# A recurrent block and an expert layer on one core: arithmetic moved off VectorE

## The reference, cut to what matters

```python
def wkv(k, v):                      # step over the 256 tokens of a sequence
    a = ew * a + exp(k_t) * v_t;  b = ew * b + exp(k_t)
    out_t = a / (b + 1e-8)
y  = layernorm(x);  xn = ln1(y)                        # two norms, one upon the other
k, v, r = mixes of (xn, shifted xn) @ Wk, Wv, Wr
x2 = y + (sigmoid(r) * wkv(k, v)) @ Wo
yn = ln2(x2);  kk = relu((yn + shifted yn) / 2 @ Wfk) ** 2
x3 = x + x2 + sigmoid(yn @ Wfr) * (kk @ Wfv)
m  = layernorm(x3);  scores = m @ gate                 # ln3
out = x3 + sum over the 2 best experts e of prob_e * w3_e(silu(h1) * h2),  h1, h2 = w12_e(m)
```

## Time and profile before

| | |
|---|---|
| median of three runs | 346.63 us (344.88 to 347.21) |
| the profiled execution | 347.12 us |
| its span, from the first to the last instruction | 345.2 us |
| busy of the span: TensorE, VectorE, GpSimd, ScalarE | 78%, 72%, 62%, 57% |
| first stage, until the last dispatch has landed | about 223 us |

### The profile page before, as it was taken

One profiled execution on the slowest core, in us unless ns is written; L12 is line 12 of the kernel. 1 busy time (PEld: TensorE's weight loads), 2 busy tenths in 40 slices (PEclk: granted clock), 3 DMA queues, 4 the chain that ended last, 5 costly groups with the idle time before them and its releaser, 6 DMA issues.

```text
span 345.2 us, 6699 instructions
## 1 busy us (share of the span) xinstructions
PE 269.8 (78%) x1697; PEld 209.4 (61%) x1698; DVE 249.8 (72%) x789; ACT 197.6 (57%) x413; POOL 215.4 (62%) x226
## 2 busy tenths in 40 slices
PE   0687599996967999695948734989999999999700
PEld 0233266673836757373745421689999999999700
DVE  3079998999889898997824648156666666666794
ACT  3546478786866588475535303366666666766200
POOL 5224356356767788588587677536666666666680
PEclk9999899999998799897896965899999999999965
DMA  8999900707162171301011211333333333333784
GB/s 273 434 316 381 353 0 2 277 4 292 41 223 92 32 293 48 93 31 61 26 39 54 70 41 47 85 90 90 94 90 88 91 90 85 84 99 92 256 313 173
DMA packets 30613, 46.11 MB, mean 134 GB/s; under 512 B 4333, under 2 KB 15599, under 8 KB 30336
## 3 DMA queue, kind: packets, MB, share of 16 engines
q1 hardware_dynamic: 23616, 30.76, 27.7%
q0 software_dynamic: 4352, 8.47, 7.4%
q10 hardware_dynamic: 2624, 6.64, 5.0%
HBM read 15.09 MB, written 29.18 MB: 128 GB/s over the span
## 4 chain that ended last, share of the span: by engine, by line
issue 30%; DVE 23%; POOL 22%; PE 5%; DMA 5%; SPq 1%; DVEq 1%; POOLq 1%; ACT 0%
POOL res_d L451 11%; POOL rows_d L426 7%; DVE st L832 4%; DVE den L883 2%; DVE rden L893 2%; DVE num L887 2%; DVE xm L937 2%; DMA o_all<-res_d 2%; DVE mv L839 2%; POOL rs L374 2%; POOL gated L389 1%; PE p_f L733 1%; DMA rows_d<-rows,pos 1%; DMA res_d<-yo,result_row 1%; DVE ekv L882 1%
## 5 line engine op out<-in xcount | busy, mean ns | idle before, releaser
L451 POOL DMA_INDIRECT res_d<-yo,result_row x72 | 71.5, 993 | 38.7 <-issue 29.6
L426 POOL DMA_INDIRECT rows_d<-rows,pos x64 | 67.3, 1052 | 22.8 <-issue 22.5
L806 PE MATMUL p_up<-xgT,w_up 128*128 128x128 f32 x576 | 70.2, 275 | 0.0
L806 PEld LDWEIGHTS p_up<-xgT,w_up 128*128 128x128 f32 x576 | 67.2, 192 | 0.0
L1062 DVE SCALAR_TENSOR_TENSOR gate_h<-th,p_up 128x512 f32<-128x512 f32 x36 | 24.8, 688 | 39.6 <-ACT th L610 39.6
L625 ACT ACTIVATE w_up<-w_exp 128x512 f32 x72 | 41.3, 622 | 10.1 <-DVE slot_w L1040 5.1
L721 PE MATMUL p_up<-ysum,w_sb 128*128 128x512 f32 x64 | 36.9, 687 | 5.3 <-POOL ysum L404 5.3
L610 ACT ACTIVATE th<-p_up 128x512 f32<-128x512 f32 x36 | 21.5, 597 | 28.1 <-PE p_up L806 28.1
L733 PEld LDWEIGHTS p_f<-wfv_half,kk 128*128 128x128 f32 x256 | 32.2, 198 | 5.3 <-issue 4.9
L733 PE MATMUL p_f<-wfv_half,kk 128*128 128x128 f32 x256 | 33.1, 283 | 0.0
L893 DVE RECIPROCAL rden<-den 128x512 f32<-128x512 f32 x8 | 26.7, 3343 | 0.0
(11 more groups left out here) (151 smaller groups left out, 550.8 us busy)
## 6 DMA issues: line engine op xcount, KB each, us to landing
rows_d<-pad SPq DMA_DIRECT2D x8, 2080.0 KB, 7.8
xg<-rows_d SPq DMA_DIRECT2D x72, 65.0 KB
o_all<-res_d SPq DMA_DIRECT2D x16, 256.0 KB, 5.2
w_exp<-experts ACTq DMA_DIRECT2D x1, 3072.0 KB, 16.9
x_all<-x SPq DMA_DIRECT2D x10, 256.0 KB, 2.4
out<-x_all ACTq DMA_DIRECT2D x8, 256.0 KB, 2.4
x_all<-x SPq DMA_DIRECT2D x1, 1536.0 KB, 15.8
res_d<-yo,result_row POOLq DMA_INDIRECT x72
```

The source lines that it names most:

```text
L426: pool.indirect_dma_start(out=rows_d[:, :], out_offset=bass.IndirectOffsetOnAxis(ap=row, axis=0), in_=rows_of[is_last(c)][:, t, k, :], in_ ...
L451: pool.indirect_dma_start(out=res_d[:, :], out_offset=bass.IndirectOffsetOnAxis(ap=row, axis=0), in_=yo[u][:, n, :], in_offset=None, bound ...
L806: mm = pe.matmul(p_up[u % 2][:, n, h * P:(h + 1) * P], w_up[u % 2][:, n, h * P:(h + 1) * P], xgT[u % 2][:, n, :], start=True, stop=True)
```

## The change

The moments' small arithmetic (neg1, var1, neg2, var2, var3) moves from VectorE to GpSimd, into the power steps. The copies in `moments` go: each `bn_aggr` now waits for its own `bn_stats`. The epsilon of den becomes a ScalarE step, `add_eps`, with a place of its own in ScalarE's order, ahead of `gate_y`. GpSimd's gated goes, and ScalarE's second instruction for tr: VectorE makes wkv = num * rden (`divided`, behind the reciprocal) and rw = (tr + 1) * wkv. `label` and `place` get by with fewer instructions; esum = 1 + egap moves to ScalarE. The loops of `pipeline` and of the first norms are written out, so that all chunk numbers are constants. Buffers that the moves need (two of each st, one mv1 for all chunks, a token_no for either place) are left out of this diff.

```diff
-            first, last = min(lags), CHUNKS - 1 + max(lags)
-            lo, hi = max(lags) + 1, CHUNKS - 1 + min(lags)
-
-            def turn(i):
+            for i in range(min(lags), CHUNKS + max(lags)):
                 for step, lag in steps:
-                    if not isinstance(i, int) or 0 <= i - lag < CHUNKS:
+                    if 0 <= i - lag < CHUNKS:
                         step(i - lag)
-
-            for i in range(first, lo):
-                turn(i)
-            with eng.Fori(lo, hi + 1) as i:
-                turn(i)
-            for i in range(hi + 1, last + 1):
-                turn(i)
...
-                pool.wait_ge(S["ln1_var"], last)
+                pool.wait_ge(S["ln1_moments"], last)
+                pool.tensor_scalar(neg1[:, part], mv1[:, part, 0], -1.0, None, ALU.mult)
+                pool.tensor_scalar(var1[:, 0, part], mv1[:, part, 1], LN_EPS, None, ALU.add)
+                pool.tensor_scalar(var1[:, 1, part], mv1[:, part, 1], 1.0 + LN_EPS, LN_EPS * LN_EPS, ALU.mult, ALU.add)\
+                    .then_inc(S["ln1_var"], 1)
+                pool.wait_ge(S["ln1_var"], n + 1)
...
+                after(pool, "ln2_moments", c + 1)
+                after(pool, "z2_ready", c)
+                pool.tensor_scalar(var2[:, :], mv2[:, :, 1], LN_EPS, None, ALU.add).then_inc(S["ln2_var"], 1)
+                pool.tensor_scalar(neg2[:, :], mv2[:, :, 0], -1.0, None, ALU.mult).then_inc(S["ln2_neg"], 1)
                 after(pool, "ln2_var", c + 1)
-                after(pool, "z2_ready", c)
                 pool.tensor_tensor(rs2[:, :], var2[:, :], neg_half[:, 0, 0:TPC], ALU.pow).then_inc(S["ln2_rstd"], 1)
+                after(pool, "ln2_neg", c + 1)
                 after(pool, "ln2_rstd", c + 1)
                 pool.tensor_tensor(nm2[:, :], rs2[:, :], neg2[:, :], ALU.mult).then_inc(S["nm2_ready"], 1)
...
-            def gate_sums(c):
-
-                after(pool, "gate_r1", c + 1)
-                after(pool, "num_ready", c + 1)
-                after(pool, "rw_ready", c)
-                pool.tensor_tensor(gated[:, :], tr[:, :], num[:, :], ALU.mult).then_inc(S["gated_ready"], 1)
...
+                after(pool, "ln3_moments", c + 1)
+                after(pool, "xm_ready", c)
+                pool.tensor_scalar(var3[:, :], mv3[:, :, 1], LN_EPS, None, ALU.add).then_inc(S["ln3_var"], 1)
                 after(pool, "ln3_var", c + 1)
-                after(pool, "xm_ready", c)
...
+            def add_eps(c):
+
+                after(act, "den_ready", c + 1)
+                act.activation(den[:, :], den[:, :], ACT.Identity, bias=wkv_eps[:, 0:1]).then_inc(S["den_eps"], 1)
+
             def tanh_r(c):
 
                 after(act, "r_done", c + 1)
-                after(act, "gated_ready", c)
+                after(act, "rw_ready", c)
                 act.activation(tr[:, :], p_r[:, :], ACT.Tanh, scale=0.5).then_inc(S["gate_r"], 1)
-                after(act, "gate_r", c + 1)
-                act.activation(tr[:, :], tr[:, :], ACT.Copy, bias=1.0).then_inc(S["gate_r1"], 1)
...
+                after(act, "egap_ready", c + 1)
+                act.activation(esum[:, :], egap[:, :], ACT.Copy, bias=1.0).then_inc(S["esum_ready"], 1)
...
-                           (first_apply, 0), (gate_y, 3), (first_norm, 2)])
+                           (first_apply, 0), (add_eps, 1), (gate_y, 3), (first_norm, 2)])
...
+                st = st[:, c % 2]
+                after(dve, which + "_moments", c - 1)
                 for t in range(TPC):
-                    last = dve.bn_stats(st[:, t, :], src(t))
-                last.then_inc(S[which + "_stats"], 1)
-                after(dve, which + "_stats", c + 1)
-
-                w = int(which[2]) - 1
-                dve.tensor_copy(moments_wait[:, w:w + 1], st[:, TPC - 1, 0:1])
+                    dve.bn_stats(st[:, t, :], src(t)).then_inc(S[which + "_stats"], 1)
                 for t in range(TPC):
-                    last = dve.bn_aggr(mv[:, t, :], st[:, t, :])
+                    after(dve, which + "_stats", c * TPC + t + 1)
+                    last = dve.bn_aggr(mv(t), st[:, t, :])
                 last.then_inc(S[which + "_moments"], 1)
-                after(dve, which + "_moments", c + 1)
...
-                moments(lambda t: x_all[:, bass.ds(c * TPC + t, 1), :].rearrange("p o d -> p (o d)"), st1, mv1, "ln1", c)
-                dve.tensor_scalar(neg1[:, tiles_of(c)], mv1[:, :, 0], -1.0, None, ALU.mult)
-
-
-                dve.tensor_scalar(var1[:, 0, tiles_of(c)], mv1[:, :, 1], LN_EPS, None, ALU.add)
-                dve.tensor_scalar(var1[:, 1, tiles_of(c)], mv1[:, :, 1], 1.0 + LN_EPS, LN_EPS * LN_EPS, ALU.mult, ALU.add)\
-                    .then_inc(S["ln1_var"], 1)
+                moments(lambda t: x_all[:, bass.ds(c * TPC + t, 1), :].rearrange("p o d -> p (o d)"), st1,
+                        lambda t: mv1[:, c * TPC + t, :], "ln1", c)
...
-                if last - first == 1:
-                    ln1(first)
-                else:
-                    with dve.Fori(first, last) as c:
-                        ln1(c)
+                for c in range(first, last):
+                    ln1(c)
...
+                after(dve, "rden_ready", c)
                 dve.tensor_tensor_scan(den[:, :], decay[:, :], ekf, 0.0, ALU.mult, ALU.add).then_inc(S["den_ready"], 1)
-                after(dve, "den_ready", c + 1)
-                dve.tensor_scalar(den[:, :], den[:, :], WKV_EPS, None, ALU.add).then_inc(S["den_eps"], 1)
                 after(dve, "ekv_ready", c + 1)
...
+            def divided(c):
+
+                after(dve, "rden_ready", c + 1)
+                after(dve, "num_ready", c + 1)
+                dve.tensor_tensor(wkv[:, :], num[:, :], rden[:, :], ALU.mult).then_inc(S["wkv_ready"], 1)
+
             def receptance(c):
 
-                after(dve, "gated_ready", c + 1)
-                after(dve, "rden_ready", c + 1)
+                after(dve, "wkv_ready", c + 1)
+                after(dve, "gate_r", c + 1)
                 after(dve, "wo_done", c)
-                dve.tensor_tensor(rw[:, :], gated[:, :], rden[:, :], ALU.mult).then_inc(S["rw_ready"], 1)
+                dve.scalar_tensor_tensor(out=rw[:, :], in0=tr[:, :], scalar=1.0, in1=wkv[:, :],
+                                         op0=ALU.add, op1=ALU.mult).then_inc(S["rw_ready"], 1)
...
-                moments(lambda t: x2[:, t, :], st2, mv2, "ln2", c)
                 after(dve, "nm2_ready", c)
-                dve.tensor_scalar(neg2[:, :], mv2[:, :, 0], -1.0, None, ALU.mult)
-                dve.tensor_scalar(var2[:, :], mv2[:, :, 1], LN_EPS, None, ALU.add).then_inc(S["ln2_var"], 1)
+                moments(lambda t: x2[:, t, :], st2, lambda t: mv2[:, t, :], "ln2", c)
...
-                moments(lambda t: x3[:, t, :], st3, mv3, "ln3", c)
                 after(dve, "ln3_rstd", c)
-                dve.tensor_scalar(var3[:, :], mv3[:, :, 1], LN_EPS, None, ALU.add).then_inc(S["ln3_var"], 1)
+                moments(lambda t: x3[:, t, :], st3, lambda t: mv3[:, t, :], "ln3", c)
...
-                for k in range(TOPK):
-                    last = dve.tensor_tensor(spots[:, k, :, :], hot[:, k, :, :], spot[:, :, :], ALU.mult)
-                last.then_inc(S["spots_ready"], 1)
+                dve.tensor_tensor(spots[:, :, :, :].rearrange("p k t e -> p k (t e)"),
+                                  hot[:, :, :, :].rearrange("p k t e -> p k (t e)"),
+                                  spot[:, :, :].rearrange("p t (o e) -> p o (t e)", o=1).to_broadcast([P, TOPK, TPC * E]),
+                                  ALU.mult).then_inc(S["spots_ready"], 1)
...
-                after(dve, "egap_ready", c + 1)
-                dve.tensor_scalar(esum[:, :], egap[:, :], 1.0, None, ALU.add).then_inc(S["esum_ready"], 1)
-
-                dve.tensor_tensor(higher[:, 0, :], low[:, 0, :], low[:, 1, :], ALU.is_lt)
-                dve.tensor_tensor(higher[:, 1, :], low[:, 1, :], low[:, 0, :], ALU.is_lt).then_inc(S["order_known"], 1)
-                after(dve, "order_known", c + 1)
-
+                dve.tensor_tensor(higher[:, :], low[:, 0, :], low[:, 1, :], ALU.is_lt).then_inc(S["order_known"], 1)
+                after(dve, "esum_ready", c + 1)
                 after_dispatched(dve, c)
                 rows = rows_of[is_last(c)]
+                dve.reciprocal(rows[:, :, 0, D + 1], esum[:, :]).then_inc(S["prob1"], 1)
+                after(dve, "order_known", c + 1)
+
                 for k in range(TOPK):
-                    last = dve.scalar_tensor_tensor(out=rows[:, :, k, D].bitcast(I32), in0=higher[:, k, :],
-                                                    scalar=float(TOKENS), in1=token_no[:, tiles_of(c)],
+                    last = dve.scalar_tensor_tensor(out=rows[:, :, k, D].bitcast(I32), in0=higher[:, :],
+                                                    scalar=float(TOKENS) * (1 - 2 * k), in1=token_no[:, k, tiles_of(c)],
```

(31 more changed lines are left out.)

2 lines of the change are left out of this document (1 added, 1 removed).

## The result

The changed kernel takes 332.05 us (median of 4 runs, 329.64 to 333.26), the kernel before in the same rounds 346.73: ratio 0.9578, 95% interval 0.9542 to 0.9614. The forecast was 334.8. The profiled execution took 332.05 (span 330.3), 15.07 less than the one before. Here is where it came from, windows cut at ln3's first instruction on GpSimd as in the earlier trace rows (busy us of PE, PEld, DVE, ACT, POOL, then granted clock, DMA share, GB/s).

A forecast was written before the change was run, and what follows sets the result against it. In the full turns GpSimd and VectorE hold each other up through the product rw. From 347.12 us, 2.8 early and 9.65 in four turns come off, 0.6 is added: 335.3, by the median 334.8, range 332 to 338.

The forecast's parts named there:

- The mechanism: VectorE's rw, no longer waiting for gated or held by GpSimd's adds, takes 0.7 us; the 2.87 us idle ahead of ln3 goes.
- Four turns: Turns with VectorE computing whole chunks and GpSimd dispatching: 19.0 us each, 76.0 against 85.65, saving 9.65.
- 0.45 by an estimate that no term of the sum below needs: VectorE's label loses three instructions of 4 columns and the waits between them: 0.45 us, counted nowhere in the sum.
- the second half's gap: GpSimd's second half of a dispatch begins 0.54 us after nm when written out, 0.16 in the loop: plus 0.38.
- divided's 0.2: VectorE's new product slows dispatch DMAs on GpSimd by between 0 and 0.6 us a turn; 0.2 taken.
- Up to the first full turn: Stretch up to 80.73 us: 11.45 saved, 8.65 given back, net 2.8 earlier, with ends 0 and 6.
- The epsilon: Moved to ScalarE: VectorE saves 0.34 us a turn, but ScalarE stands some 2.7 for den and x2 waits 0.85.
- the moved collision: Rival: spots and seen held through all three GpSimd adds, turn 20.2 us, total 339.6; chance 0.20.
- Behind the turns: After 166.38 us: two ln2 instructions and one ln3 instruction more on GpSimd, no gated there to save: plus 0.6.
- the bound on ScalarE and TensorE: Rival: the epsilon stall and a lower TensorE clock stretch ranks by 3 us, turn 21, total 342.8; chance 0.10.
- the dear GpSimd: Rival: GpSimd's new instructions cost what its power costs, 0.82 us dearer each, 351.5 by the median; chance 0.05.
- a free place: Rival: VectorE is ahead of the adds throughout and place is never held, turn 18.1 us, total 331.2; chance 0.07.

The follow-up runs named there:

- gate_back: Changed kernel with gated on GpSimd again, tr made in two instructions and rw = gated * rden: 344.37 us, ratio to before 0.9962.
- adds_after_rw: Kernel before with one wait added, GpSimd's add_ffn waiting until rw of the same moment is made: 341.85 us, ratio to before 0.9879.
- label_back: Changed kernel with label as before (esum on VectorE, two comparisons, reciprocal and a copy): 333.01 us, ratio to before 0.9645.
- gate_alone: Kernel before with only the gate folded into VectorE's last product, no gated on GpSimd: 341.82 us, ratio to before 0.9879.
- eps_late: Changed kernel with ScalarE's epsilon step behind first_norm instead of ahead of gate_y: 329.47 us; 330.91 in a repeat with an ineffective added wait.
- eps_back: Changed kernel with the epsilon on VectorE again, between den and num, and no such ScalarE step: 335.60 us, ratio to before 0.9671.

## Why the prediction was right

**The mechanism** was right: rw at 0.7 us, no idle ahead of ln3, GpSimd and VectorE about equal in the turn. gate_back and adds_after_rw show it from both sides.

**Four turns**: 76.0 forecast, 73.3 measured; this is the term that was mis-sized most. The forecast took GpSimd's 18.8 us as its own work. In it were a gap of 0.82 us ahead of the first dispatch DMA and that DMA's 1.63; now, in the turn shown, they are 0.20 and 1.17, 1.08 us that no part of the sum held. The 1.63 is the scan den, as label_back shows. The gap I had read as issue; by the rows it was a wait for label: in six places of the kernel before the DMA starts 0.98 to 0.99 us after label's last instruction, and in label_back 0.99. So "0.45 by an estimate that no term of the sum below needs" was the wrong step: undoing label costs 0.46 us a turn. These 0.46 come from the longer DMA. The gap itself opens by only 0.03 us without the label's change and by 0.10 without the moments', as in either case label still ends 0.68 us or more ahead of the power's end, 0.17 in the kernel before; no run undoes both. The other terms came as forecast: gated away, 0.23 us for each new instruction, 0.55 for the second half's gap, 0.18 of waiting for moments. divided's 0.2 was not seen: the DMAs beside it take 0.97 to 1.09, and 1.08 at 162.10 without it. The prediction drew a cost of up to 0.6 a turn from the Trainium skill ("SBUF — State Buffer", "Who interferes with whom"). The same section reports that a DMA was not stalled beside a `tensor_tensor`; the trace agrees with that. Two things that the sum had at nothing go the other way: add_ffn beside rw takes 1.54 us in place of 1.29, and GpSimd waits 0.42 for yn. With them 19.0 - 1.08 - 0.2 + 0.25 + 0.42 = 18.4, the length of the turn shown.

**Up to the first full turn**: 2.8 forecast, 0.97 measured, though x came 0.94 us later in this execution (18.59, 17.65 before), so 1.9 from x on, in one execution each; the early part of the same kernel differs by up to 2.2 us between two. The terms that pull it down were those named: divided (0.67 a chunk in gate_alone) and the stall at the epsilon, which delays x2 by up to 1.84 us; eps_late, which takes the stall away, wins 3.1 and 5.6 us here in its two pairs.

**The epsilon** was counted as a saving on VectorE that a wait takes back. In the full turns the wait is as forecast (x2 stands 0.58 to 0.71 us a turn, 0.85 said), released by TensorE's p_tok and not by y1 as the prediction's signs have it. But undoing the step costs 2.1 us in four turns, not nothing.

Why the moved collision stayed away in the changed kernel is open. The reason that I gave, the one add each of the earlier trace rows, is not enough, since in eps_back spots is held through three. The 0.42 us of waiting for yn are not enough either: in the changed kernel's last full turn ysum follows add_ffn at once, and spots gets in all the same.

```profile
149.27 1.46 POOL L390 TENSOR_TENSOR x<-ffn,x_all 128x512 f32<-128x512 f32 x1
150.70 1.03 POOL L397 TENSOR_TENSOR ysum<-yn 128x512 f32<-128x512 f32 x1
```

```profile
149.75 1.07 DVE L973 TENSOR_TENSOR spots<-hot,spot 128x64 f32<-128x64 f32 x1
```

What differs by the rows is the start: in the changed kernel's full turns add_ffn begins beside rw, and spots 0.48 to 1.24 us behind add_ffn's start; in eps_back add_ffn begins behind rw and spots within 0.06 us of it. The stall on ScalarE or the epsilon's own time on VectorE may bring this about; no run parts the two.

**Behind the turns** +0.6 was forecast and -1.03 measured. The same gap ahead of a dispatch (0.20 in place of 0.70 us) lies in the stretch three times. label_back has it at 0.33 to 0.36 there and takes no longer from rw of chunk 7 on than the changed kernel (60.01 and 60.00), so label by itself is not what wins here; the rest is not tested.

**The rivals**: the bound on ScalarE and TensorE did not come (clock 1.00 in the turns); the dear GpSimd neither; place was held in one of the turns' ends only (at 149.75, 1.07 and 1.01 us), so the time is near the case of a free place (331.2). Its turn of 18.1 us could not follow from a free place, though, as the prediction's own sum has GpSimd at 18.6; the 1.08 above made the 18.3 of the four turns possible.

**The total** was 335.3 for the profiled execution and 332.05 measured. The four turns won 2.7 us more than forecast, the stretch behind them 1.6, the expert stage and the time around the span 0.7; the early part won 1.8 less. That this last miss takes back part of the others is luck.

## What to carry to other kernels

When an instruction takes several times its usual duration, look at what the other engine of the pair runs just then, and ask which edit lets it start elsewhere; moving it may only pass the collision on to the next product, as in eps_back. Edits that are worth little alone can be worth much together when one uncovers the bound that the other relieves, so undo parts in the changed kernel as well as trying them alone. Before adding a wait, look where the semaphore's count starts.

## What the hardware showed unasked

A VectorE product was held through a whole row of GpSimd adds, not through one: 3.53 to 3.96 us in place of 0.2 to 0.7, over three adds of 1.29, 1.05 and 1.27 us. In other turns it was let in when the first add ended, with the next one close behind (149.75 in the changed kernel); what decides is not shown. The hold also works the other way: a dispatch DMA on GpSimd that meets the scan den ends 0.84 to 1.06 us after the scan does, and so takes up to 1.84 us; in the three dispatches behind the turns, with no scan beside it, the first DMA takes 1.04 to 1.17, and most of the others take 0.97. An "issue" gap of 0.70 to 0.82 us ahead of an indirect DMA hid a wait: in six places of the kernel before, the DMA starts 0.98 to 0.99 us after the last instruction of label, which it waits for.
